# A mixture-of-experts sweep whose last weight part is split in the piece that uses it

## The reference, cut to what matters

```
topk_ids = argmax(x @ gate_w)                       # one expert for each token
sorted_x = (x * sigmoid(topk_val))[argsort(topk_ids)]
g = ragged_dot(sorted_x, routed_gate_w, tokens_per_expert)   # 32 x (512 x 1024)
u = ragged_dot(sorted_x, routed_up_w, tokens_per_expert)
d = ragged_dot(silu(g) * u, routed_down_w, tokens_per_expert) # 32 x (1024 x 512)
```

## Time and profile before

| | |
|---|---|
| median of 3 runs | 3889.35 us (3884.31 to 3890.14) |
| the profiled execution's own time | 3882.45 us |
| its span, first to last instruction | 3880.8 us |
| mean granted TensorE clock | 0.993 |
| TensorE busy with matmuls | 3813.0 us, 98% |
| VectorE, ScalarE, GpSimd busy | 54%, 52%, 19% |

### The profile page before, as it was taken

How to read it: one execution, slowest core, us unless ns; L and a number is a source line. 1 busy time by engine, 2 the same in 40 slices (tenths; PEclk the granted TensorE clock), 3 DMA queues, 4 the chain that set the end, 5 groups by cost and what they waited for, 6 DMA issues and landing times.

```text
span 3880.8 us, 57690 instructions
## 1 busy us (share of the span) xinstructions
PE 3813.0 (98%) x19358; PEld 3271.0 (84%) x19359; DVE 2106.0 (54%) x3199; ACT 2007.8 (52%) x2860; POOL 723.3 (19%) x841
## 2 busy tenths in 40 slices
PE   8999999999999999999999999989999999999998
PEld 6888888888877888888888888878999999999997
DVE  5332323333256555555555555566667767677674
ACT  3222222222237767677676767754455556565553
POOL 2011010101115100000000000022333334343333
PEclk9999999999999999999999999999999999999999
DMA  5222222222121100000110000066666768687673
GB/s 172 90 90 100 92 89 84 92 100 92 74 77 55 52 33 33 32 32 32 44 53 32 32 32 33 22 241 222 224 223 234 274 213 278 233 274 254 221 271 125
DMA packets 309383, 481.11 MB, mean 124 GB/s; under 512 B 32570, under 2 KB 208827, under 8 KB 305476
## 3 DMA queue, kind: packets, MB, share of 16 engines
q1 hardware_dynamic: 271700, 361.19, 26.9%
q0 software_dynamic: 37616, 119.08, 8.9%
HBM read 364.73 MB, written 102.99 MB: 121 GB/s over the span
## 4 chain that ended last, share of the span: by engine, by line
PE 65%; DVE 2%; issue 2%; ACT 1%; DVEq 1%; DMA 0%; ACTq 0%; SPq 0%; POOLq 0%; POOL 0%
PE bank L87 15%; PE bank L89 15%; PE bank L88 15%; PE bank L1828 11%; PE bank L1205 6%; PE bank L1209 3%; PE bank L1778 1%; DVE yo L1726 0%; DVEq L1347 0%; DVE wlo L1474 0%; DVE th L1708 0%; DVE hs L1088 0%; ACT L1055 0%; ACT w_hi L93 0%; DVE yo L1722 0%
## 5 line engine op out<-in xcount | busy, mean ns | idle before, releaser
L87 PE MATMUL bank<-txT,whi 128*128 128x256 f32 (+2 forms) x2048 | 612.5, 299 | 8.9 <-ACT tsg L1608 4.5
L89 PE MATMUL bank<-txT,wlo 128*128 128x256 f32 (+2 forms) x2048 | 608.3, 297 | 0.0
L88 PE MATMUL bank<-txT,whi 128*128 128x256 f32 (+2 forms) x2048 | 608.2, 297 | 0.0
L87 PE MATMUL bank<-xT,w_hi 128*128 128x512 f32 x1536 | 598.3, 390 | 0.0
L88 PE MATMUL bank<-xT,w_hi 128*128 128x512 f32 x1536 | 598.0, 389 | 0.0
L89 PE MATMUL bank<-xT,w_lo 128*128 128x512 f32 x1536 | 598.0, 389 | 0.0
L1474 DVE TENSOR_TENSOR wlo<-raw,whi 128x1024 fp32r<-128x1024 f32 x372 | 445.8, 1220 | 40.7 <-ACT whi L1469 40.7
L1828 PE MATMUL bank<-whi,thT 128*128 128x512 f32 x1264 | 412.4, 397 | 10.3 <-issue 10.3
L648 DVE TENSOR_TENSOR h_act<-h_act,psU 128x512 f32<-128x512 f32 x128 | 88.1, 688 | 607.4 <-PE psU L89 607.3
L1469 ACT ACTIVATE whi<-raw 128x1024 fp32r<-128x1024 f32 x372 | 384.1, 1050 | 35.8 <-DMA raw<-in_L_ffn_routed_down_w 19.7
L87 PEld LDWEIGHTS bank<-txT,whi 128*128 128x128 f32 x2048 | 389.3, 190 | 13.5 <-DVE th L1708 5.2
(11 more groups left out here) (213 smaller groups left out, 7596.4 us busy)
## 6 DMA issues: line engine op xcount, KB each, us to landing
raw<-in_L_ffn_routed_gate_w SPq DMA_DIRECT2D x124, 512.0 KB, 3.8
raw<-in_L_ffn_routed_up_w SPq DMA_DIRECT2D x124, 512.0 KB, 5.3
raw<-in_L_ffn_routed_down_w SPq DMA_DIRECT2D x124, 512.0 KB, 5.6
xT_dram<-xT SPq DMA_DIRECT2D x16, 2048.0 KB, 6.3
xT<-xT_dram SPq DMA_DIRECT2D x14, 2048.0 KB, 8.1
xs_dram<-x_in SPq DMA_DIRECT2D x16, 1024.0 KB, 4.3
ss_dram<-y_sb SPq DMA_DIRECT2D x64, 256.0 KB, 2.0
ss_dram<-ry SPq DMA_DIRECT2D x64, 256.0 KB, 2.1
```

The lines of the kernel that those rows point to most:

```text
L87: pe.matmul(out, w[0], x[0], start=start, stop=False)
L88: pe.matmul(out, w[0], x[1], start=False, stop=False)
L89: return pe.matmul(out, w[1], x[0], start=False, stop=stop)
```

## The change

For the experts 1 to 31, D1 is no longer split at the end of the expert before. It is split in the expert's own last piece, if no full piece is ahead of it: the first half after block 0, the second after block 1, by ScalarE and then by VectorE. If there are full pieces, it is split before the first of them. ScalarE's wait for `y_mm` of the piece before, which guards whi and wlo of D1, moves with it. Expert 0 is split as before. TensorE's, GpSimd's and SyncE's programs are the same; SyncE's wait for `wlo_done` of D1 ahead of the load of part 2 is met at another time.

```diff
             def expert(e, split):
...
                 with eng.If(full > 0):
-                    if first:
-                        for q in OWN:
-                            own(q)
+                    for q in OWN if first else (D1,):
+                        own(q, e, p)
                     with eng.Fori(0, MOST) as i:
                         with eng.If(full > i):
-                            piece(p + i, e, MOST_UNITS, False, None)
-                piece(p + full, e, n, split, full if first else None)
+                            piece(p + i, e, MOST_UNITS, False, False, None)
+                piece(p + full, e, n, split, first, full)
...
-        def own_part(eng, own, q, full):
+        def own_part(eng, own, q, e, p, full, halves=(0, 1)):
 
             with eng.If(full < 1):
-                own(q)
+                own(q, e, p, halves)
...
-            def own(q):
-                split_hi(act, q, 0)
+            def own(q, e=0, p=0, halves=(0, 1)):
+                if halves[0] == 0 and not (isinstance(e, int) and e == 0):
+                    for g in range(GROUPS):
+                        act.wait_ge(y_mm[g], p + 1)
+                split_hi(act, q, e, halves)
...
                     h_hi(b)
                     if first and b in (0, 2, 4):
-                        own_part(act, own, OWN[b // 2], full)
+                        own_part(act, own, OWN[b // 2], e, p, full)
+                    if not first and full is not None and b < 2:
+                        own_part(act, own, D1, e, p, full, (b,))
...
                 third(act, n, lambda: gated(2), lambda: act.sem_inc(zs_done[2], 1))
-                hi(D1)
...
-            def own(q):
-                split_lo(dve, q, 0)
+            def own(q, e=0, p=0, halves=(0, 1)):
+                split_lo(dve, q, e, halves)
...
                     h_lo(b)
                     if first and b in (0, 2, 4):
-                        own_part(dve, own, OWN[b // 2], full)
+                        own_part(dve, own, OWN[b // 2], e, p, full)
+                    if not first and full is not None and b < 2:
+                        own_part(dve, own, D1, e, p, full, (b,))
...
                 third(dve, n, last, absent)
-                lo(D1)
```

More of the change, by code:

```diff
@@ L1602, in _, with piece @@
                 own(q)
-            def piece(p, e, n, split, full):
+            def piece(p, e, n, split, first, full):
                 def silu(b):
@@ L1624, in hi @@
                             act.wait_ge(u_mm, p * NI + 2 * q + 2)
-                        elif q == D0:
+                        else:
                             act.wait_ge(d0_mm, p * 2 + 4)
-                        else:
-                            for g in range(GROUPS):
-                                act.wait_ge(y_mm[g], p + 2)
                         split_hi(act, q, e + 1, halves)
-                first = full is not None
                 for b in range(NI):
```

## The result

Four runs of the changed kernel gave 3916.17 us in the median (3913.05 to 3918.8), four of the kernel before beside them 3888.4. The ratio is 1.0072, with a 95% interval from 1.0058 to 1.0085: 27.8 us slower. The forecast was 3921, so +31.6. The profiled execution took 3913.05 us, its span is 3911.4, 30.6 more than before's 3880.8.

A forecast was written before the change was run, and what follows sets the result against it. TensorE, busy for 98% of the span, was taken as the bound. Sixteen 256-column pieces at 2.3 us (+36.8) less 5.2 of old waits gave +31.6: 3889.35 + 31.6 = 3921 us, range 3896 to 3945.

The forecast's parts named there:

- Removed: D1's split at the end of the piece ahead: lies beneath the expert loop's turn; first `th` stays about 6.4 us, nothing won.
- Added: Half splits in blocks 0 and 1 of 256-column pieces: VectorE's chain comes 3.24 us later, not 2.28.
- Blocks 3 and 4: TensorE's up blocks 3 and 4 in 256-column pieces: 0.6 us late, with small waits for VectorE's `th`.
- The turn: TensorE's `turn_x(p+1, 1)` for the next piece, after `x_lo(p+1, 0)` in bank psX: 1.9 us late.
- The sum: Whole kernel: 16 pieces of 256 columns at 2.3 us, +36.8, less 5.2 of old waits: +31.6.
- No cost on the queues: SP's queue: part 2's load waits for D1's split, D0's goes 3.0 us later; taken as nothing, at most 8 us.
- 320 and 384 columns: Larger pieces: VectorE catches up by block 5 at 320 columns; no loss there, and none at 384.
- Rival 1: Loop's turn isn't beneath the split: first `th` at about 4.1 to 4.8 us; -7.5 us, 3882; chance 0.14.
- Rival 2: Each half costs VectorE's chain only 1.14 us: 1.5 us per 256-column piece, +19, 3908; chance 0.14.
- Rival 3: The granted clock falls too after TensorE's gaps of 1.3 to 1.6 us: +18 us more, 3939; chance 0.10.
- Rival 4: TensorE has room for all of the moved work: time within 0.2%; chance 0.04.

## Why the prediction was right, point by point

**Removed: nothing won.** Right. 6.42 and 6.26 to 6.30 against a forecast of 6.4 for both (three pieces behind late data of D0 had 6.7 to 7.0), and the run without the splits shows the floor by itself. From the last `yo` to the first `th` it is 3.57 and 3.58 us, with and without 2.36 us of work in it. The Trainium skill (Advanced Engine Details and Errata, Sequencer Loop) says that engine instructions can be queued while control instructions execute. The trace agrees with that.

**Added: 3.24 for the chain.** Right: steps of 3.32 and 3.23 where 3.32 and 3.24 stood.

**Blocks 3 and 4.** 0.6 was forecast. In the sample TensorE is 0.8 late at the turn of group 0 (20.97, before 20.16); behind three groups it is 0.65. The waits are put down to `tsg` more than to `th` (the gate's bank goes free with `tsg`, which queues behind h hi and the half's rounding on ScalarE). Place and size right, the named releaser half right.

**The turn.** 1.9 was forecast and 2.17 measured: the chain's end is 28.33 and not 28.1. It is 3.19 later, not 3.0: `th` 7 is 3.08 later, and the `txT` behind it starts 0.75 us after it instead of 0.64, where the sum had taken 0.2 off for x_hi. Behind the turn 0.47 was lost against 0.4 to 0.5. Per piece that is 2.64, and 2.3 to 2.6 where a third group is turned, against 2.4 and 2.2.

**The sum.** Fifteen pieces at 2.3, less 4.8 of the old waits, would be 29.7; they gave 32.84. Against undisturbed pieces (34.87 and 35.36) these fifteen were 4.9 us too long before and 37.7 now. So the old waits did come off in full, and the price of a piece was sized too low: 2.5 and not 2.3. About 1.2 of the 3 us is the later landing of D0, which the sum took at nothing: in three pieces the results and the next first `th` came 0.3 to 0.5 later. The sixteenth gave 2.08. Then about 4 us came back ahead of and in the pieces of experts 0 and 2, which the sum had at nothing. Expert 2's gap is only 1.46 of its 2.75: in the two stretches of 3 us behind the gap the granted clock was 0.63 and 0.80, and in the kernel before it was 0.50 in both, so the gap's length is paid a second time by the clock. These first pieces differ by several us in all nine traces, expert 2's by 0.8 to 2.9 less than in the kernel before in every one of the others. With one execution each, it isn't shown whether the edit has a part in it. The total of 30.65 in the profile is thus the forecast's 31.6 with two errors of 3 and 4 us in opposite directions. That it lies so near is luck in part. The mechanism, and the price of a piece within a tenth, are not.

**No cost on the queues.** Nearly right: D0's load went out 24.2 us into the piece and not 21.2, and ScalarE's waits for down parts were 14.1 us in 14, before 19.7 in 14. But 4.9 us in 7 of waits for up parts are new, and the 1.2 us named above belong here. The margin is small: the kernels with the rounding first and with the shorter turn lost 1 to 3 us in several pieces to part 3's data.

**320 and 384 columns.** Right: -0.10 and -0.03 over all of them.

**The rivals.** Rival 1 (faster) is refuted by the kernel without the splits and by the one with them whole behind the turn; what VectorE had unsaturated was the turn and ScalarE's replies, which this spreading of the splits could not fill. The Trainium skill (Perfetto Trace Analysis, Optimizing Scalar/DVE Operations) says only that breaking up instructions may let work be done sooner where Vector isn't saturated. Here the halves stayed whole instructions and were placed apart, and the time rose by the ratio 1.0072, so the time that the prediction drew from that sentence did not come. Rival 2 (1.14 a half) is refuted as to this kernel, by the steps of 3.3; where the rounding comes first and the steps are 2.8, the undisturbed pieces lost 1.1 to 1.5, its 1.5 or somewhat less (36.23 - 34.87 = 1.36, 36.52 - 35.36 = 1.16). Rival 3 (the clock) is refuted: gaps of up to 1.2 us at the turn, and 1.00 granted in both windows. Even gaps of 2.5 us and 2.6 us at this place in the kernels with the rounding first and the shorter turn were followed by 1.00. Rival 4 (hidden) is refuted by the interval from 1.0058.

## What to carry to other kernels

A loop's turn that reads words into registers costs an engine time in which queued work can run, so work ahead of the turn may be free where the same work behind it is paid in full: look for the distance from the last hand-over to the first instruction behind the turn, and not at the idle time, which the work hides. Before spreading work over a chain that crosses two engines, price each share with the exchange it adds (here 1.14 us of work became 1.62), and compare the chain with the bounding engine's pace block by block. And where a chain was made shorter, late data took back a part of it (15.6 and 19.7 us of waits): check which load is next to be late.

## What the runs showed of the hardware that was not expected

Reading a word into a register is dear: the three reads of VectorE's turn take 2.2 of the 2.7 to 2.9 us for which VectorE stands idle there in the kernel after, some 0.7 each, and one read less, with its branches, gave back 1.2 us.

Waits for up parts, of which the kernel before has none from 2600 on, are there in the kernel after (4.9 us) and more so in the two with a shorter chain (15.6 and 19.7) and the one with the turns later (11.6), though the 16 DMA engines had a mean busy share of only 0.69 to 0.77 in four pieces with late data. In the two kernels that split D1 earlier or half of it (whole behind the turn, one half in each place) there are none. Why was not tried.

TensorE shows gaps of several us put down to "issue" at the down products of experts 0 and 2 (5.30 and 4.98 before, 5.31 and 3.52 after) and none like them later. Expert 0 has the first piece of 256 columns and expert 2 the first of 320; expert 4, with the first of 384, shows no gap. The queue that the profile calls "instruction" (q8) moved packets in the pieces of these two experts, in both gaps of the kernel before, and none from 2690 to 3860. That TensorE waits there for code that it runs for the first time is thus a guess and was not tried. Behind these gaps the granted clock was 0.50 for at least 3 us (0.63 behind the shortest, 3.52).
